# Attention row maxima: one transpose a pair over folded key lanes, by way of DRAM, in place of four

## The reference, cut to what matters

```python
s = jnp.einsum('bthd,bshd->bhts', q, k) * scale
logits = DEG * jnp.log(jnp.abs(s) + 1e-30) + log_G[:, :, :, None] - log_G[:, :, None, :]
mask = jnp.tril(jnp.ones((T, T), dtype=bool))
logits = jnp.where(mask, logits, -jnp.inf)
m = jax.lax.stop_gradient(jnp.max(logits, axis=-1, keepdims=True))
a = jnp.exp(logits - m)
num = jnp.einsum('bhts,bshd->bthd', a, v)
den = jnp.sum(a, axis=-1).transpose(0, 2, 1)
y = num / (den[..., None] + 1e-06)
```

## Time and profile before

| | us |
|---|---|
| median of three runs (lowest, highest) | 2114.95 (2114.72, 2115.79) |
| the profiled execution, its own time | 2115.08 |
| its span | 2113.3 |
| attention, from its first matmul to its last reduction | 263 to 1295 |
| busy in the span: TensorE, VectorE, ScalarE, GpSimd | 1937.4, 1786.6, 1305.3, 806.1 |

### The profile page before, as it was taken

How to read it: one execution, slowest core, us unless ns; L and a number is a source line. 1 busy time by engine, 2 the same in 40 slices (tenths; PEclk the granted TensorE clock), 3 DMA queues, 4 the chain that set the end, 5 groups by cost and what they waited for, 6 DMA issues and landing times. The chain is left out here.

```text
span 2113.3 us, 37841 instructions
## 1 busy us (share of the span) xinstructions
PE 1937.4 (92%) x13191; PEld 1378.1 (65%) x13191; DVE 1786.6 (85%) x2777; ACT 1305.3 (62%) x2216; POOL 806.1 (38%) x701
## 2 busy tenths in 40 slices
PE   7999779999999999999999996999727999999993
PEld 5767535555555555555555553899627999999993
DVE  6999849999999999999999997777576778787783
ACT  4454357777777787777787773444325656566661
POOL 3777611121111112111111210566505666656563
PEclk9999889999999999999999998999857999999997
DMA  5887892355543345543335502344333344334444
GB/s 189 281 276 270 268 247 60 92 130 125 125 96 104 84 117 125 130 118 81 101 96 125 130 16 83 106 131 132 124 119 78 73 89 87 72 80 89 89 91 109
DMA packets 160216, 261.06 MB, mean 124 GB/s; under 512 B 48680, under 2 KB 124272, under 8 KB 153584
## 3 DMA queue, kind: packets, MB, share of 16 engines
q1 hardware_dynamic: 131904, 214.20, 36.2%
q0 software_dynamic: 15840, 22.66, 6.7%
q10 hardware_dynamic: 12304, 22.02, 3.3%
HBM read 162.77 MB, written 100.27 MB: 124 GB/s over the span
## 5 line engine op out<-in xcount | busy, mean ns | idle before, releaser
L999 ACT ACTIVATE att_sb_a<-att_ps_s,att_sb_fg,att_sb_f 128x1024 f32<-128x1024 f32 x384 | 454.3, 1202 | 230.0 <-PE att_ps_s L1144 218.9
L1037 DVE TENSOR_TENSOR keep_sb_store<-keep_sb_store,att_sb_a 128x1024 f32<-128x1024 f32 (+2 forms) x528 | 535.0, 1027 | 16.3 <-ACT att_sb_a L999 7.9
L955 POOL TENSOR_SCALAR_AFFINE_SELECT att_sb_dec<-att_sb_dec 128x128 f32<-128x128 f32 x256 | 178.5, 698 | 844.3 <-ACT att_sb_dec L989 844.3
L1163 PE MATMUL att_ps_off<-att_sb_a,att_sb_v 128*64 128x512 f32 x1520 | 365.5, 594 | 1.2 <-DVE att_sb_part L1064 1.1
L1835 ACT ACTIVATE ffn_sb_h<-ffn_ps_p,ffn_sb_b_cols 128x256 f32<-128x256 f32 x320 | 152.0, 476 | 170.1 <-PE ffn_ps_p L2015 169.6
L1144 PE MATMUL att_ps_s<-att_sb_q,att_sb_k 64*128 64x512 f32 (+1 forms) x1896 | 229.7, 376 | 5.0 <-DMA att_sb_k<-k_rows 4.8
L1144 PEld LDWEIGHTS att_ps_s<-att_sb_q,att_sb_k 64*128 64x128 f32 x1896 | 158.9, 186 | 115.0 <-issue 64.1
L1144 PEld LDWEIGHTS att_ps_s<-keep_sb_late,att_sb_k 64*128 64x128 f32 x1920 | 160.4, 185 | 110.1 <-issue 56.6
L1144 PE MATMUL att_ps_s<-keep_sb_late,att_sb_k 64*128 64x512 f32 (+3 forms) x1920 | 230.8, 374 | 0.3
L1934 DVE TENSOR_TENSOR ffn_sb_h_lo<-ffn_sb_h,ffn_sb_h_hi 128x256 fp32r<-128x256 f32 x320 | 211.4, 707 | 22.0 <-ACT ffn_sb_h_hi L1828 21.0
L1053 DVE SCALAR_TENSOR_TENSOR att_sb_a<-att_ps_s,att_sb_dec 128x1024 f32<-128x1024 f32 (+3 forms) x256 | 208.9, 816 | 7.8 <-PE att_ps_s L1144 5.3
(11 more groups left out here) (253 smaller groups left out, 3565.9 us busy)
## 6 DMA issues: line engine op xcount, KB each, us to landing
q_rows<-early_sb_halves SPq DMA_DIRECT2D x32, 1024.0 KB, 4.9
att_sb_k<-k_rows SPq DMA_DIRECT2D x60, 512.0 KB, 15.8
keep_sb_raw<-L_ffn_W ACTq DMA_DIRECT2D x36, 512.0 KB, 4.0
close_sb_nT<-num_rows SPq DMA_DIRECT2D x34, 512.0 KB, 4.0
k_rows<-early_sb_halves SPq DMA_DIRECT2D x16, 1024.0 KB, 4.9
keep_sb_late<-q_rows SPq DMA_DIRECT2D x32, 512.0 KB, 13.6
num_rows<-att_sb_num SPq DMA_DIRECT2D x64, 256.0 KB, 2.5
att_sb_hb<-half_log SPq DMA_DIRECT2D x15, 1024.0 KB, 22.7
```

Source lines behind the costliest of these rows:

```text
L955: nc.gpsimd.affine_select(out=tile, in_=tile, compare_op=ALU.is_ge, fill=0.0, base=0, pattern=[[1, P]], channel_multiplier=-1).then_inc(de ...
L999: nc.scalar.activation(x, s_ps[slot(op)][:, :, :], ACT.Square, scale=f[:, p, i - 1, s:s + 1], bias=fg[:, p, i - 1, s:s + 1]).then_inc(sq_d ...
L1037: nc.vector.tensor_tensor(x[:, :, c:TB], x[:, :, c:TB], y[:, :, c:TB], ALU.max).then_inc(max_done, 1)
L1163: last = nc.tensor.matmul(ps[h * HD:(h + 1) * HD, c:TB], v_tile, a[:, a_slot(op), h, c:TB], start=(s == 0), stop=(s == (ST * i if kind == ...
```

## The change

1. `PATTERN` has one max step a pair (`x0`, 40 steps and this one: 41 places), carried into the next round, where it had four. Only the last pair keeps its four steps; they get places of their own in the closing round.
2. When a block's maximum is complete, SyncE stores `acc[:, i]` (512 KB) to a new DRAM tensor `top_rows[q, i]`. From there 16 loads of 32 partitions (128 KB each) bring it back: buffer `tops[0]` receives lanes 0 to 31 of all four blocks (block i on partitions 32 i to 32 i + 31), and `tops[1]` receives, one after the other, lanes 32 to 63, 64 to 95 and 96 to 127.
3. VectorE joins `tops[1]` into `tops[0]` three times (`fold`, 128 x 1,024 each). TensorE transposes `tops[0]` in eight pieces, and two reductions (one for each head, 512 elements to 16) write the pair's whole `row_max`.
4. A block's running maximum isn't begun anew before its store for the last pair has landed (`top_st`).
5. The loads of pair q+2 are cut by blocks of queries and keys into four parts of eight DMAs of 128 KB (with the values and `hb` in the third), and lie between the new stores and loads in SyncE's list.
6. The constants of the other engines' orders are new, and so is the order of the off and diag steps.
7. Two buffers of a later stage (`keep.raw`) are placed after the attention's memory has been freed; their first load was behind the attention before, too.

```diff
-PATTERN = ("d3 o1 o1 d3 o1 d3 d3 o1 o2 o2 o2 d1 o2 x0 x3 "
-           "o2 d1 o2 o2 d1 o2 d1 o3 d2 o3 o3 d2 d2 o3 o3 "
-           "d2 d0 o3 x1 o3 o3 o3 o3 d0 d0 x2 d0 o3 o3")
-CARRIED = ("d3", "x3", "x0")
+PATTERN = ("d3 o1 o1 d3 o1 d3 o1 d3 o2 o2 d1 o2 d1 o2 "
+           "d1 o2 o2 o2 o2 d1 o3 d2 d2 o3 o3 d2 o3 d2 "
+           "d0 o3 o3 d0 o3 o3 d0 o3 o3 o3 d0 x0 o3")
+CARRIED = ("d3", "x0")
+FOLDS = (0.58, 0.71, 0.86)
...
+    def fold_at(q, n):
+        return (q + 1 + FOLDS[n - 1]) * N
...
+    sp_todo = [(values_at(last_own(q, i)) + 1, "num", (q, i)) for q, i in owns]
+    sp_todo += [(max_at(last_own(q, i)) + 1, "top", (q, i)) for q, i in owns if q < PAIRS - 1]
+    sp_todo += [(fold_at(q, 1) - 5, "tops", (q, 0)) for q in range(PAIRS - 1)]
+    sp_todo += [(fold_at(q, n - 1) + 1 if n > 1 else fold_at(q, 1) - 5, "tops", (q, n)) for q, n in folds]
+    sp_todo += [(values_at(last_own(q, 3)) + 1.01 + at, "pair", (q + 2, i))
+                for q in range(PAIRS - 2) for i, at in enumerate((0, 10, 16, 22))]
...
-        FIRST_PART, FIRST_SOME, FIRST_REST, LOADS = 16 * 9, 16 * 8, 16 * 12, 16 * 9
+        FIRST_PART, FIRST_SOME, FIRST_REST, LOADS = 16 * 9, 16 * 8, 16 * 12, 16 * (8 * NB + 1)
...
-            def load(q):
-                load_scored(sp, q_sb[q % 2], k_sb[q % 2], q_rows, k_rows, q // KVH, q % KVH, slice(0, NB), slice(0, NB), pair_in[q % 2])
-                load_values(sp, q // KVH, q % KVH, v_cent, v_sb[q % 2], pair_in[q % 2])
-                load_logs(q)
+            def load(q, i):
+                at = slice(i, i + 1)
+                load_scored(sp, q_sb[q % 2][:, at], k_sb[q % 2][:, at], q_rows, k_rows, q // KVH, q % KVH, at, at, pair_in[q % 2])
+                if i == 2:
+                    load_values(sp, q // KVH, q % KVH, v_cent, v_sb[q % 2], pair_in[q % 2])
+                    load_logs(q)
...
+            def store_top(q, i):
+                sp.wait_ge(max_done, max_order.count(last_own(q, i)))
+                sp.dma_start(top_rows[q, i], acc[:, i, :, :].rearrange("p h c -> p (h c)")).then_inc(top_st[i], 16)
+
+            def load_tops(q, n):
+
+                if n == 0:
+                    for i in range(NB):
+                        sp.wait_ge(top_st[i], 16 * (q + 1))
+                    if q:
+                        sp.wait_ge(s_done, s_order.count((q - 1, "max", 0, 0)))
+                elif n == 1:
+                    if q:
+                        sp.wait_ge(fold_done, 3 * q)
+                else:
+                    sp.wait_ge(fold_done, 3 * q + n - 1)
+                for i in range(NB):
+                    sp.dma_start(tops[n > 0][i * FOLD:(i + 1) * FOLD, :], top_rows[q, i, n * FOLD:(n + 1) * FOLD, :]).then_inc(tops_in[n > 0], 16)
...
+                if q and s == (0 if i == 0 else 1):
+                    dve.wait_ge(top_st[i], 16 * q)
...
+            def fold(q, n):
+                x, y = tops
+                if n == 1:
+                    dve.wait_ge(tops_in[0], 16 * NB * (q + 1))
+                else:
+                    dve.wait_ge(fold_done, 3 * q + n - 1)
+                dve.wait_ge(tops_in[1], 16 * NB * (3 * q + n))
+                nc.vector.tensor_tensor(x[:, :], x[:, :], y[:, :], ALU.max).then_inc(fold_done, 1)
...
+                for h in range(2):
+                    last = nc.vector.tensor_reduce(keep.row_max[:, q, :, h].rearrange("p (i c) -> p c i", c=ST),
+                                                   s_ps[slot(op)][:, h, :].rearrange("p (c i k) -> p c i k", c=ST, k=FOLD), AX.X, ALU.max)
+                last.then_inc(row_done, 1)
```

More of the change, by code:

```diff
@@ L762, in attention_places @@
             q = body - carried
-            if 0 <= q < PAIRS:
+            if 0 <= q < PAIRS - (kind == "max"):
                 place[q, kind, i, s] = body * N + n
+    last = PAIRS - 1
+    for s, i in enumerate((1, 2, 0)):
+        place[last, "max", i, 0] = place[last, "diag", 3, s + 1] + 0.4
+    place[last, "max", 3, 0] = place[last, "diag", 3, ST - 1] + 8
     return N, place
@@ L795, in __iter__, with attend @@
         return iter(self.ops)
[L798 removed]
+def attend(nc, keep, early, first, used_up, store, late, q_rows, k_rows, v_cent, half_log, num_rows, top_rows):
     N, place = attention_places()
@@ L839, in attend @@
+    total_order = Order({(q, i): values_at(last_own(q, i)) - 0.82 for q, i in owns})
     slots = Order({op: place[op] for op in offs + diags})
+    folds = [(q, n) for q in range(PAIRS - 1) for n in range(1, ST)]
+    def fold_at(q, n):
+        return (q + 1 + FOLDS[n - 1]) * N
     pe_todo = [(place[op], "s", op) for op in place] + [(values_at(op), "av", op) for op in offs + diags]
-    act_todo = [(place[op] + (0 if op[1] == "off" else 2.96), "sq", op) for op in offs + diags]
-    act_todo += [(place[op] - 5.95, "dec", op) for op in diags]
@@ L844, in attend @@
-    act_todo += [(place[q, "off", i, 0] - 1.18, "et", (q, i)) for q, i in blocks]
-    act_todo += [(q * N + N * 0.88, "factors", (q + 1,)) for q in range(PAIRS - 1)]
+    act_todo = [(place[op] + (0 if op[1] == "off" else 2.81), "sq", op) for op in offs + diags]
+    act_todo += [(place[op] - 2.09, "dec", op) for op in diags]
+    act_todo += [(place[q, "off", i, 0] - 1.64, "et", (q, i)) for q, i in blocks]
+    act_todo += [(q * N + N * 0.92, "factors", (q + 1,)) for q in range(PAIRS - 1)]
     dve_todo = [(max_at(op), "max", op) for op in offs + diags]
-    dve_todo += [(place[op] + 0.34, "own", op) for op in diags]
@@ L1090, in _ @@
                     scale(*op)
+                elif what == "fold":
+                    fold(*op)
                 elif what == "part":
@@ L2208, in build @@
                 used_up = project(nc, keep, early, first, rows, dr["L0_attn_x"], q_rows, k_rows, v_cent, gate_logit, half_log)
-            attend(nc, keep, early, first, used_up, store, late, q_rows, k_rows, v_cent, half_log, num_rows)
+            attend(nc, keep, early, first, used_up, store, late, q_rows, k_rows, v_cent, half_log, num_rows, top_rows)
+        keep.raw = [m.sbuf(f"raw{i}", [P, KD * INNER // 2]) for i in range(2)]
         h2_rows = scratch("h2_rows", (NTT, P, D + TAG))
```

67 lines of the change are left out of this document (45 added, 22 removed).

## The result

| | before | changed kernel |
|---|---|---|
| median of four runs, us | 2115.37 | 2164.76 |
| lowest, highest | 2114.72, 2115.89 | 2163.38, 2170.58 |
| profiled execution, its own time; span | 2115.08; 2113.3 | 2163.38; 2161.6 |

The changed kernel is slower: ratio 1.0239, with a 95% interval of 1.022 to 1.0258. Forecast were 2119 us and a range up to 2142; the measured time lies above it. All times are medians of executions in the fast state, which leaves one out: 2750.5 us at a granted clock of 0.65, of the run that keeps only the waits.

A forecast was written before the change was run, and what follows sets the result against it. TensorE bounds the kernel, VectorE 4% behind; afterwards a load loop through the second fold. From 2115.1: - 2.0 - 3.6 + 1.0 + 14 x (63.4 - 62.8) = 8.8, so 2119 us; range 2084 to 2142.

The forecast's parts named there:

- What the engines allow: TensorE and VectorE together: 61.0 us a pair, between 60.2 and 62.0, VectorE becoming the slower engine.
- the first rival: Pair loads come in time and the engines set 61.0 us a pair: 2086 us, chance 0.21, faster.
- The wait that takes over: TensorE idle 3 to 5 us once a pair, before the tile following `x0`, waiting for the pair's loads.
- the loop: First tile through numerator, second fold and the queued loads behind it to the next first tile: 63.4 us a pair.
- Step 1: From a pair's first tile to VectorE's first numerator, two score tiles and a product with the values: 2.0 us.
- Step 2: From the first numerator to the second fold, 45 VectorE instructions of 39.5 us plus 0.5 idle: 40.0 us.
- Steps 3 to 5: Second fold 1.2 us, queue behind it up to part four 18.6, issue and landing latency 1.6.
- Sum: Loop steps 2.0 + 40.0 + 1.2 + 18.6 + 1.6 = 63.4 us a pair, giving 2119 us.
- The one order of SyncE: SyncE's list in each pair: parts three and four of the loads stand behind the second fold's reload.
- The first fold: Reload before the first fold: 13.8 us of VectorE work covers 13.5 us of queue, cover 0.3 us.
- the second rival: Narrow loads below some 208 GB/s make the first fold wait too: 65.0 us a pair, 2142 us, chance 0.21, slower.
- ScalarE's wait for `hb`: `hb` lands 13 us behind the second fold, ScalarE arrives at about 11: a 2 us delay costing nothing.

The follow-up runs named there:

- the run that keeps only the waits: Changed kernel without stores and reloads of the maxima for pairs 1 to 14, SyncE still waiting for the first and second fold; 2094.4 us, ratio 0.991.
- The last run: Changed kernel with pair-load parts one and two issued after the last score tile, parts three and four left where they were; 2147.6 us, ratio 1.0153.
- the run without the traffic: Changed kernel without stores and reloads of the maxima for pairs 1 to 14 and without SyncE's waits for the folds; 2083.1 us, ratio 0.9842.
- the fastest one: Changed kernel with pair-load parts one and two issued after the last score tile, three and four moved up to the places of two and three; 2082.9 us.
- the run with interleaved halves: Changed kernel with pair loads over 64 partitions, the two halves of a head interleaved so the memory side begins with 32 rows; 2169.8 us, ratio 1.0267.

## Why the prediction was wrong, step by step

**What the engines allow**, 61.0 us: right. Without the traffic the time is 2083 us, the first rival's 2086; with the loads moved the period is 60.7.

**The wait that takes over**, right in place, and in cause as far as it goes: the loads behind the second fold, before the tile that follows `x0`, 4.3 to 5.7 us (3 to 5 forecast), but in nine rounds and not in fourteen. The last run confirms the loop. That the queue behind the first fold is nearly as long stands nowhere in the forecast.

**Step 1**, 2.0 us: wrong, 3.45. It was priced with the tiles of the earlier trace rows, at a clock of 1.00, though the step ahead of it was a forecast wait of several microseconds. This is the step that failed most: 1.45 us in a loop of nine rounds. With TensorE kept busy in the wait it is 2.08, as forecast, and 21 us of the time come back (9 to 22 by the spread), so the excess is the lower clock.

**Step 2**, 40.0: 41.4. VectorE's instructions were right (39.95 us busy from 670.54 to 711.92, 39.5 forecast); its idle time was 1.4 instead of 0.5. The low clock is not the reason: with TensorE kept busy in the wait the step still takes 41.2 to 41.6 us in four of five rounds, 42.3 in the fifth. That TensorE is late is the reason, as far as the runs show it: in the same kind of round the step takes 39.7 us where TensorE didn't wait (the run without the traffic and the fastest one), and 40.4 to 41.3, growing with the wait, behind waits of 0.8 to 1.8 us after which the tiles ran at full speed (the run that keeps only the waits). A TensorE with less lead over VectorE would do this; that step is not shown apart.

**Steps 3 to 5**, 21.4: 21.8. Price by width, latency, SyncE's 24 issues: right within 2% in this round (21.7 to 22.6 in the four rounds of its kind that are followed by another wait). The narrow loads ran at about the assumed 215 (216 GB/s at full share in 717 to 721; 221 and 225 in 676 to 680 of the fastest run).

**Sum**: the steps missed 1.45 + 1.4 + 0.4 = 3.2 us of a round. 2119 + 14 x 3.2 = 2164, the measured 2163 of the profiled run. That the sum closes is partly luck, since only five of the nine rounds that wait are of the kind that was priced, and five more go by another path. Their length is nearly the same: three cycles of three rounds from 466.11 on take 201.0 to 201.9 us, one 196.5.

**The one order of SyncE**: wrong in one pair of three as to parts two and three, in another as to part two. Only a round of the first kind was read. The slip didn't make the forecast too low: with one order in all rounds the kernel is 18 us slower still.

**The first fold**: its cover was given as 0.3 us, and the second rival said that it would wait. It waits in nine rounds, 9.8 us, without the narrow loads being slow: the rival's condition (under 208 GB/s) did not come, its mechanism partly did. In that rival the fold's wait came before the loop; that the queue behind the first fold is itself a second loop was not seen.

**The range**: both ends were worked out at a clock of 1.00 and with at most 1 us of idle time in step 2. The upper end was the second rival's 65.0 us; the two terms that were missed, together 2.9 us over the 63.4 of the sum, lie outside it.

**ScalarE's wait for `hb`**, forecast as 2 us and free: it comes in nine rounds, 1.7 to 4.0 us, and VectorE waits 9.9 us in all for decay tiles that GpSimd finishes. No run tested it apart; whether the one comes from the other, and whether it costs something, stays open.

## What to carry to other kernels

Where a forecast ends in a wait of TensorE, price what follows it at the lower clock, and count the lead of the other engines from there. A queue that is issued in order has a limit behind each of its blocking waits, all that stands between that wait and the first use of the last transfer; price every one of them before moving anything, since shortening one alone gained little here (folds earlier: 2170.7 and 2163.6; parts one and two out of the first fold's way, the second's loop as it was: 2147.6; less behind both folds: 2082.9). Look at the stretches where the DMA engines stand idle inside the busy part: they name the wait that holds. Then look for the earliest moment at which a buffer is really free: here the last score, not the last product.

## What was not expected of the hardware

A wait of 4.4 us halved the granted clock (0.50 in 668 to 670). Shorter ones did both: after 2.24 us, before 592.29, eight transposes took 1.94 us instead of 1.09, while after the 2.42 us before 726.06, with 3.7 us of transposes ahead of them, the tiles ran at full speed, and so did eight transposes after 2.86 us of standing still (1.06 us, before 394.36 of the run with interleaved halves). A DMA whose memory side begins with a dimension of 2 ran on 2 of 16 engines, 53 GB/s, and held up the queue behind it. 64 partitions gave 199 GB/s, no more than 32.
